# Reordering the last stage of a fused pair-update and mixture-of-experts kernel: transposes by halves, an earlier gate, a later bias

## What is computed

```
a    = layernorm(layernorm(x))
left = mask * (a @ Wl.T + bl) * sigmoid(a @ Wlg.T + blg)        # right likewise
t    = einsum('ikc,jkc->ijc', left, right);  t = layernorm(t)
x    = x + (t @ Wo.T + bo) * sigmoid(a @ Wg.T + bg)
p    = softmax(layernorm(x) @ router_w + router_b)              # 8 experts
top2 = the two largest p, divided by their sum
x    = x + sum over the top2 of p_e * (layernorm(x) @ expert_w[e] + expert_b[e])
```

## Time and profile before

| what | value |
|---|---|
| median of 3 runs | 1064.48 us (1064.04 to 1065.31) |
| the profiled execution | 1064.93 us |
| its span, first to last instruction | 1063.1 us |
| busy over the span: TensorE, VectorE, GpSimd, ScalarE | 90%, 78%, 62%, 42% |
| mean granted TensorE clock | 0.972 |
| first `turns` of stage C | at 342.7 us |
| last `total` | at 1058.5 us |

### The profile page before, as it was taken

How to read it: one execution, slowest core, us unless ns; L and a number is a source line. 1 busy time by engine, 2 the same in 40 slices (tenths; PEclk the granted TensorE clock), 3 DMA queues, 4 the chain that set the end, 5 groups by cost and what they waited for, 6 DMA issues and landing times.

```text
span 1063.1 us, 20940 instructions
## 1 busy us (share of the span) xinstructions
PE 957.2 (90%) x6712; PEld 545.5 (51%) x6712; DVE 829.9 (78%) x2945; ACT 448.5 (42%) x842; POOL 661.0 (62%) x632
## 2 busy tenths in 40 slices
PE   4798999979999689999999999999999999999986
PEld 3566666768886444444444444444444444444432
DVE  4899999831224678888888888888888888888883
ACT  1465566611111234444444444444444444444433
POOL 5997888432221137676767676767676767676654
PEclk9999999989999569999999999999999999999999
DMA  7678777989980123242424242423242423242331
GB/s 186 199 255 280 277 260 250 349 274 312 301 255 31 31 74 97 80 121 80 120 81 119 80 119 81 120 80 120 80 120 80 120 81 120 80 119 80 100 90 59
DMA packets 119390, 153.07 MB, mean 144 GB/s; under 512 B 10486, under 2 KB 76278, under 8 KB 117238
## 3 DMA queue, kind: packets, MB, share of 16 engines
q1 hardware_dynamic: 118150, 151.32, 46.2%
q10 hardware_dynamic: 1136, 0.46, 0.2%
HBM read 67.33 MB, written 50.33 MB: 111 GB/s over the span
## 4 chain that ended last, share of the span: by engine, by line
PE 44%; DVE 42%; issue 6%; POOL 5%; DMA 1%; ACT 1%; SPq 0%; POOLq 0%; DVEq 0%
PE b_m L773 13%; PE ein L666 11%; DVE zb L997 8%; PE gt L706 6%; PE ring L760 6%; DVE stage L834 6%; DVE bst_x L1046 4%; PE pr_a L629 4%; DVE sig_c L1006 3%; DVE x2t L1013 3%; DVE bst L821 3%; DVE bst_t L895 2%; POOL xs L378 1%; POOL xs L382 1%; PE xt_a L617 1%
## 5 line engine op out<-in xcount | busy, mean ns | idle before, releaser
L442 POOL TENSOR_TENSOR zb<-bcs,x2d 128x512 f32<-128x512 f32 x256 | 326.6, 1276 | 216.3 <-ACT bcs L549 162.9
L773 PE MATMUL b_m<-zb,w_exp 128*64 128x512 f32 x1024 | 258.7, 614 | 1.1 <-POOL zb L442 1.1
L549 ACT ACTIVATE bcs<-ring 128x512 f32<-128x512 f32 x256 | 153.7, 601 | 208.0 <-PE ring L760 202.0
L997 DVE TENSOR_TENSOR zb<-ring,x2d 128x512 f32<-128x512 f32 x256 | 175.7, 686 | 57.6 <-PE ring L760 57.0
L834 DVE SCALAR_TENSOR_TENSOR stage<-pr_a,mt,sig_a 128x128 f32<-128x128 f32 x512 | 148.0, 420 | 11.2 <-ACT sig_a L493 11.2
L760 PE MATMUL ring<-wt,sel 64*128 64x512 f32 x512 | 128.3, 498 | 26.8 <-DVE zb L997 26.6
L629 PE MATMUL pr_a<-w_proj,xts 64*128 64x256 f32 x1024 | 139.3, 402 | 14.4 <-DVE stage L834 13.9
L427 POOL TENSOR_TENSOR tn<-t_all,rr 128x512 f32<-128x512 f32 x64 | 85.8, 1340 | 60.8 <-PE gt L687 32.8
L773 PEld LDWEIGHTS b_m<-zb,w_exp 128*64 128x64 f32 x1024 | 57.7, 135 | 119.8 <-issue 95.2
L629 PEld LDWEIGHTS pr_a<-w_proj,xts 64*128 64x128 f32 x1024 | 96.1, 191 | 43.0 <-issue 22.1
L493 ACT ACTIVATE sig_a<-pr_a 128x512 f32<-128x512 f32 x128 | 76.4, 597 | 72.1 <-PE pr_a L629 72.0
(11 more groups left out here) (132 smaller groups left out, 1495.7 us busy)
## 6 DMA issues: line engine op xcount, KB each, us to landing
left_right_scratch<-stage SPq DMA_DIRECT2D x16, 2048.0 KB, 7.6
x2d<-x2t SPq DMA_DIRECT2D x256, 128.0 KB, 2.8
chunk<-left_right_scratch SPq DMA_DIRECT2D x24, 1024.0 KB, 9.0
xc<-in_x SPq DMA_DIRECT2D x64, 256.0 KB, 3.1
out<-outc SPq DMA_DIRECT2D x64, 256.0 KB, 2.1
chunk<-left_right_scratch SPq DMA_DIRECT2D x12, 384.0 KB, 8.1
chunk<-left_right_scratch SPq DMA_DIRECT2D x8, 192.0 KB, 5.4
chunk<-left_right_scratch SPq DMA_DIRECT2D x4, 256.0 KB, 8.0
```

The lines of the kernel that those rows point to most:

```text
L442: pool.tensor_tensor(zb[:, tile_buffer(u, m), :], bcs[:, n % 2, :], x2d[:, u % 2, m % 2, :], ALU.mult)\
L549: act.activation(bcs[:, n % 2, :], ring[:, m % 2, :], ACT.Copy).then_inc(bcast_out, 1)
L773: ins = pe.matmul(b_m[rows[t], :], w_exp[:, ep, :], zb[:, tile_buffer(u, 2 * ep + t), :], start=ep == 0, stop=ep == EP - 1, skip_group_che ...
L997: dve.tensor_tensor(zb[:, tile_buffer(u, m), :], ring[:, m % 2, :], x2d[:, u % 2, m % 2, :], ALU.mult).then_inc(z_dve, 1)
```

## The change

All transposes of the last stage are done by halves of 64 partitions, half `r` into bank `r` of the target, as `turns` does already: `x_turn` (into `gt`), `y_turn` and `pack_turn` (now both into `b_d`, the latter behind `back`'s results in it). The readers (`residual`, `y_evacuate`, `pack`) read both banks. `turns` no longer waits for the pack; `y_turn`, `pack_turn` and `back` get the waits that the shared `b_d` needs.

TensorE's new order in slot `u` is: bcast 2, 3; back(v-1); x_turn(v); bcast 4, 5; expert 0, 1; in odd slots pack_turn; bcast 6, 7; turns(n); y_turn(u-1); bcast 0, 1 of `u+1`; bias; out_gate(n); expert 2, 3. So `out_gate(n)` stands ahead of the last two experts, and ScalarE's `gate(n)` and VectorE's `gated(n)` now run at the end of the same slot, no longer in the next one; `x_turn(v)` waits for `gated(v)`.

GpSimd: norm_x(n); scale 3, 5; norm_t(n+1); scale 7; scale 1 of `u+1`. ScalarE: bcast 3, 5; pack; bcast 7; copies(n); soft; bcast 1 of `u+1`; gate(n); y_evacuate(u-1).

VectorE in even slots: scale 2; route 1; back 1; route 2; back 0; route 3; scale 4; route 4; back 3; route 5; residual(v); route 6; back 2; scale 6; logits; route 7 to 10; bn 2; route 11; bn 3; route 12; scale 0; route 13; bn 0; route 14; bn 1; route 15; gated(v+1); route 16; total. In odd slots: route 17; scale 2; back 3; route 18; back 2; route 19; back 1; back 0; scale 4; route 20; logits; residual(v); rstd 1, 0, 2; scale 6; rstd 3 to 8; scale 0; bn 0, 3; rstd 9 to 11; bn 1, 2; gated(v+1); rstd 12; total. Its list in the diff below is cut, since this is all of it.

```diff
@@ -453,15 +453,15 @@
             ins.then_inc(sel_made, 1)
             for u in range(-LEAD - 1, UNITS):
                 n = u + LEAD + 1
+                if has(n) and n >= NX:
+                    norm_x(n)
                 if has(u):
                     scale(3, u)
                     scale(5, u)
-                if has(n) and n >= NX:
-                    norm_x(n)
+                if has(n + 1):
+                    norm_t(n + 1)
                 if has(u):
                     scale(7, u)
-                if has(n + 1):
-                    norm_t(n + 1)
                 if has(u + 1):
                     scale(1, u + 1)
 
@@ -519,12 +519,13 @@
                 chunk_b(c)
 
 
+            by_half = lambda ap: ap.rearrange("p (j r k) -> p r j k", j=JP, r=2)
+            by_bank = lambda ap: ap.rearrange("p r (j k) -> p r j k", j=JP)
+
             def copies(n):
                 act.wait_ge(turns_ready, n + 1)
                 if n >= 1:
                     act.wait_ge(og_ready, n)
-                by_half = lambda ap: ap.rearrange("p (j r k) -> p r j k", j=JP, r=2)
-                by_bank = lambda ap: ap.rearrange("p r (j k) -> p r j k", j=JP)
                 act.activation(by_half(xtn[:, :]), by_bank(gt[:, :, 0:N]), ACT.Copy)
                 act.activation(by_half(ttn[:, :]), by_bank(gt[:, :, N:2 * N]), ACT.Copy).then_inc(turns_out, 1)
 
@@ -539,7 +540,7 @@
                 h = u % 2
                 if u >= 2:
                     act.wait_ge(out_stored[h], u // 2 * 16)
-                act.activation(outc[:, h, :, :].rearrange("p j c -> p (j c)"), b_d[:, 0, :], ACT.Copy).then_inc(y_out, 1)
+                act.activation(outc[:, h, :, :].rearrange("p (j t) c -> p t j c", t=2), by_bank(b_d[:, :, 0:N]), ACT.Copy).then_inc(y_out, 1)
 
             def bcast(m, u):
                 n = tiles_before(POOL_TILES, u, m)
@@ -555,26 +556,25 @@
 
             def pack(s):
                 act.wait_ge(pack_turned, s + 1)
-                act.activation(wt[:, s % 2, :], gt[:, 1, :], ACT.Copy).then_inc(pack_out, 1)
+                act.activation(by_half(wt[:, s % 2, :]), by_bank(b_d[:, :, N:2 * N]), ACT.Copy).then_inc(pack_out, 1)
 
             for u in range(-LEAD - 1, UNITS + 1):
                 v, n = u + LEAD, u + LEAD + 1
                 if has(u):
                     bcast(3, u)
-                if has(v):
-                    gate(v)
-                if has(u):
                     bcast(5, u)
-                if u % 2 == 0 and has(u + 2):
-                    soft((u + 2) // 2)
                 if u % 2 == 1 and has(u + 1):
                     pack((u + 1) // 2)
                 if has(u):
                     bcast(7, u)
                 if has(n):
                     copies(n)
+                if u % 2 == 0 and has(u + 2):
+                    soft((u + 2) // 2)
                 if has(u + 1):
                     bcast(1, u + 1)
+                if has(n):
+                    gate(n)
                 if has(u - 1):
                     y_evacuate(u - 1)
 
@@ -683,21 +683,18 @@
             pairs = [slice(j * P, j * P + P) for j in range(JP)]
             rows = [slice(r * C, r * C + C) for r in range(2)]
 
-            def turn_half(bank, at, src):
-                return pe.transpose(gt[:, bank, at:at + C], src, ident[rows[bank], rows[bank]])
+            def turn_half(dst, r, at, src):
+                return pe.transpose(dst[:, r, at:at + C], src, ident[rows[r], rows[r]])
 
             def turns(n):
                 pe.wait_ge(norm_ready, n + 1)
                 pe.wait_ge(x_norm, n + 1)
                 if n >= 1:
                     pe.wait_ge(x2_ready, n)
-                u = n - LEAD - 1
-                if u % 2 == 1 and has(u + 1):
-                    pe.wait_ge(pack_out, (u + 1) // 2 + 1)
                 for part, src in enumerate((xn, tn)):
                     for j in range(JP):
                         for r in range(2):
-                            m = turn_half(r, part * N + j * C, src[rows[r], 2 * j:2 * j + 2, :].rearrange("p j c -> p (j c)"))
+                            m = turn_half(gt, r, part * N + j * C, src[rows[r], 2 * j:2 * j + 2, :].rearrange("p j c -> p (j c)"))
                 m.then_inc(turns_ready, 1)
 
             def out_gate(n):
@@ -709,9 +706,10 @@
                 o.then_inc(og_ready, 1)
 
             def x_turn(v):
-                pe.wait_ge(gate_ready, v + 1)
+                pe.wait_ge(om_done, v + 1)
                 for j in range(JP):
-                    m = pe.transpose(gt[:, 0, pairs[j]], xc[:, v % XC, 2 * j:2 * j + 2, :].rearrange("p j c -> p (j c)"), ident)
+                    for r in range(2):
+                        m = turn_half(gt, r, j * C, xc[rows[r], v % XC, 2 * j:2 * j + 2, :].rearrange("p j c -> p (j c)"))
                 m.then_inc(x_turned, 1)
 
             def y_turn(u):
@@ -719,16 +717,21 @@
                 pe.wait_ge(back_done, min(u + LEAD + 1, UNITS))
                 if u >= 1:
                     pe.wait_ge(y_out, u)
+                if u % 2 == 0 and has(u + 2):
+                    pe.wait_ge(pack_out, u // 2 + 2)
                 for j in range(JP):
-                    m = pe.transpose(b_d[:, 0, pairs[j]], x2t[:, u % X2, pairs[j]], ident)
+                    for r in range(2):
+                        m = turn_half(b_d, r, j * C, x2t[rows[r], u % X2, pairs[j]])
                 m.then_inc(y_turned, 1)
 
             def pack_turn(s):
                 pe.wait_ge(pick_step, (s + 1) * PICK_OPS)
-                pe.wait_ge(om_done, min(2 * s + LEAD, UNITS))
+                pe.wait_ge(back_done, min(2 * s + LEAD - 1, UNITS))
+                if s >= 2:
+                    pe.wait_ge(y_out, 2 * s - 2)
                 for j in range(JP):
-                    m = pe.transpose(gt[:, 1, pairs[j]],
-                                     pk[:, 4 * j:4 * j + 4, :, :].bitcast(F32).rearrange("p t z n -> p (t z n)"), ident)
+                    for r in range(2):
+                        m = turn_half(b_d, r, N + j * C, pk[rows[r], 4 * j:4 * j + 4, :, :].bitcast(F32).rearrange("p t z n -> p (t z n)"))
                 m.then_inc(pack_turned, 1)
 
             def back(w):
@@ -737,6 +740,8 @@
                     pe.wait_ge(back_done, w)
                 if has(w - LEAD - 1):
                     pe.wait_ge(y_out, w - LEAD)
+                elif w == LEAD - 1:
+                    pe.wait_ge(pack_out, 1)
                 for j in range(JP):
                     for t in range(2):
                         m = pe.matmul(b_d[:, t, j * BACK:(j + 1) * BACK], x2t[rows[t], w % X2, pairs[j]], route[rows[t], :],
@@ -781,32 +786,32 @@
                     bcast(3, u)
                 if has(v - 1):
                     back(v - 1)
+                if has(v):
+                    x_turn(v)
                 if has(u):
                     bcast(4, u)
                     bcast(5, u)
                     expert(0, u)
                     expert(1, u)
-                if has(v):
-                    x_turn(v)
                 if u % 2 == 1 and has(u + 1):
                     pack_turn((u + 1) // 2)
-                if has(u):
-                    bias(u)
-                if has(u - 1):
-                    y_turn(u - 1)
                 if has(u):
                     bcast(6, u)
                     bcast(7, u)
                 if has(n):
                     turns(n)
+                if has(u - 1):
+                    y_turn(u - 1)
                 if has(u + 1):
                     bcast(0, u + 1)
                     bcast(1, u + 1)
                 if has(u):
+                    bias(u)
+                if has(n):
+                    out_gate(n)
+                if has(u):
                     expert(2, u)
                     expert(3, u)
-                if has(n):
-                    out_gate(n)
 
 
         @block.vector
@@ -1005,12 +1010,15 @@
                 dve.wait_ge(og_ready, v + 1)
                 dve.scalar_tensor_tensor(sig_c[:, :], gt[:, 1, :], og_bias[:, 1:2], sig_c[:, :], ALU.add, ALU.mult).then_inc(om_done, 1)
 
+            by_half = lambda ap: ap.rearrange("p (j r k) -> p r j k", j=JP, r=2)
+            by_bank = lambda ap: ap.rearrange("p r (j k) -> p r j k", j=JP)
+
             def residual(v):
                 dve.wait_ge(om_done, v + 1)
                 dve.wait_ge(x_turned, v + 1)
                 if v >= X2:
                     dve.wait_ge(y_turned, v - X2 + 1)
-                dve.tensor_tensor(x2t[:, v % X2, :], gt[:, 0, :], sig_c[:, :], ALU.add).then_inc(x2_ready, 1)
+                dve.tensor_tensor(by_half(x2t[:, v % X2, :]), by_bank(gt[:, :, 0:N]), by_half(sig_c[:, :]), ALU.add).then_inc(x2_ready, 1)
 
             def norm_x(v):
                 dve.wait_ge(xc_in[v % XC], v // XC * 16 + 16)
...
```

More of the change, by code:

```diff
@@ L890, in _, with stats_t @@
             dve.wait_ge(ein_dve, C // 2)
-            def stats_t(s, js):
+            def stats_t(s, js, last):
                 for j in js:
```

(146 more changed lines are left out.)

9 lines of the change are left out of this document (4 added, 5 removed).

## The result

The changed kernel takes 1006.22 us (median of 4 runs, 1005.70 to 1007.34) against 1064.89 before, a ratio of 0.945 (95% interval 0.9434 to 0.9467). 1003.5 was predicted, with a range of 993 to 1025. The span of its profiled execution is 1004.3 us, 58.8 less: 1.0 up to slot 1, 54.1 in slots 1 to 57, 3.7 from slot 58 on.

The account below looks back on a forecast made before the run. TensorE and VectorE, both nearly full, wait for each other in turn. Slots of 9.61 for 10.63 us save 58 over 57 slots, the last five 3: 1063.1 - 61 + 1.8 = 1003.9, less 0.45: 1003.5, range 993 to 1025.

Parts of the forecast that it names:

- The loop: Stage C, once a slot: TensorE takes 3.84 us from tile 6 read to tile 2 ready, VectorE's scale 2 to 6 the rest, 6.3.
- The walk of a slot: Step-by-step timing of TensorE and VectorE in an even and an odd slot: 19.22 us per pair, 9.61 a slot against 10.63.
- The copies: ScalarE's copies ahead of out_gate: done by 6.2 and 6.7 us against 6.76, hidden, in odd slots with nothing to spare.
- Halves: x_turn, y_turn and pack_turn on TensorE: 0.25 us each by halves against 0.41 to 0.56 whole, removing 0.55 us per slot.
- The rival's price: Halves do not overlap: eight loads one behind another, 0.84 us a transpose instead of 0.25, 1088 us in all; chance 0.04.
- Two banks: VectorE's residual reading two banks: unchanged at 0.68 us, the lower bound; upper bound 1.36.
- VectorE 2% from the bound: VectorE's busy time, 9.39 us per slot, leaves the forecast slot of 9.61 only 2% above it.
- the 96 put down as a sign: Sign listed in the prediction: VectorE over 96% busy, with no idle before scale 2.
- the rival did not come in: VectorE becomes the bound: dearer residual or dependent small steps make a slot 9.8 to 10.1 us, 1014 to 1031; chance 0.25.
- Covers: Work on other engines expected hidden: norm_t by 0.7 us, norm_x ahead of scale 3 by 0.4, doublings with slack 1.3.
- TensorE's wait before y_turn: Sign: TensorE idle before y_turn in even slots, some 0.6 us, and hardly elsewhere.
- wait that was named as a sign of being wrong: A new wait in every slot: TensorE for GpSimd's zb or the copies, or VectorE before scale 0 for transfers.

Follow-up runs that it names:

- the old list: The changed kernel with VectorE's old order of work put back, only gated(v+1) kept ahead of total: 1113.05 us, ratio 1.0451.
- the halves alone: The kernel before with all transposes by halves and their waits, every order as it was: 1088.69 us, ratio 1.0224.
- the late gate: The changed kernel with out_gate behind experts 2, 3, gate and gated in the next slot, x_turn behind experts 0, 1: 1096.36 us, ratio 1.0290.
- the early bias: The changed kernel with the bias ahead of bcast 6, 7 again: 1031.80 us, ratio 0.9685.
- GpSimd's old list: The changed kernel with GpSimd's order scale 3, 5, norm_x, scale 7, norm_t, scale 1: 1022.78 us, ratio 0.9598.
- the logits moved: The changed kernel with logits ahead of scale 6 in even slots: 999.17 us, ratio 0.9382.
- the new list: The changed kernel, VectorE reordered: even slots residual behind route 4, logits ahead of scale 6, statistics between small steps; odd scale 2 first, statistics between rstd: 1001.47 us.

## Why the prediction was right

- **The loop.** That VectorE's work between scale 2 and scale 6, with TensorE's piece behind it, set a slot before is shown by the old list (slots of 11.0 and 10.8 when it is put back) and by y_turn alone by halves (3 us of 17). The order makes most of the gain (with x_turn and y_turn whole the kernel is already at 1028), and in it their halves are worth 22 us.
- **The walk of a slot.** For even and odd slots 9.64 and 9.58 were walked and 9.65 and 9.70 measured, 9.68 over slots 1 to 57: 54 us for 58. In even slots two terms ahead of y_turn were each 0.10 too long (bcast 2, 3 with back 1.18, not 1.28; experts 0, 1 1.87, not 1.97), which is lost again in the waits: turns wait for residual, which the walk had in time by 0.06, and y_turn waits for the logits, whose end was right (5.31 for 5.35). In odd slots the walk is 0.12 short. Rows of TensorE's timeline, then of ScalarE's: the copy of tile 7, which stands behind the pack in its list:

```profile
694.59 0.58 PE L765 MATMUL ring<-wt,sel 64*128 64x512 f32 x2
695.10 0.50 PE L770 MATMUL b_m<-wt,bias_hi 128*128 128x512 f32 x1
```

```profile
694.03 0.59 ACT L550 ACTIVATE bcs<-ring 128x512 f32<-128x512 f32 x1
```

bcast 1 needs that copy, ended at 694.62, so bcast 0, 1 take 0.51 to the next start and not 0.43; the walk had only tile 6 there. The bias adds 0.04 in both slots (0.66 to 0.67, not 0.62). The copies, called hidden "with nothing to spare", do release out_gate last in odd slots, but it starts no later behind the bias than in even ones. Ahead of slot 1 1.0 was gained where 0 was put down, and from slot 58 to the end 3.7 for 3.
- **Luck.** The total came within 2.7 us, but five of the eleven expectations of the runs above, worked out in the same way, missed by 14 to 59 us (the halves alone, the old list, the late gate, the early bias, GpSimd's old list). They had left out a new wait, a lateness handed on to the next slot, or the clock. In the change itself the waits that the walk had missed are only 0.1 to 0.2 us each, and partly fall where TensorE waits anyway. That so small an error was left is luck in part.
- **Halves.** 0.25 was right (0.25 to 0.28). The Trainium skill ("TensorE: Matmul & The Clock Gate", LDWEIGHTS) prices a load by its columns, not its rows, and the trace agrees: one load takes 138 ns at 64 rows and 140 at 128. The rival's price, eight loads one behind another, is not seen, and the overlap of other row groups that the page allows (Part 3, The mechanism) is.
- **Two banks.** residual 683 ns against 681: the lower bound, as taken.
- **VectorE 2% from the bound.** It is 95.8% busy, a little under the 96 put down as a sign, and the rival did not come in: with the logits moved a slot still got 0.14 shorter on average (9.54). It is near, though. With the logits ahead VectorE idles only 0.28 a pair of slots in the stretch read (714.62), and each reordering that made it later in one slot paid in the next (the bias, the new list).
- **Covers.** norm_t is hidden, as walked, and so are the doublings. That norm_x stood ahead of scale 3 was walked as harmless; it is worth 16.6 us, and the prediction did not say so. Nor did it see that all the halves, with pack_turn's move to `b_d`, cost 23 us without the new order. Of the other signs, TensorE's wait before y_turn is 0.37, not some 0.6, and no wait that was named as a sign of being wrong stands on TensorE or VectorE in the slots shown.

## What to carry to other kernels

When two engines are each 90% full, look in the chain for the loop between them, and move everything that has slack to the other side of it; savings inside one engine's idle time bring little until then (3 us of 17 here), and about their full price afterwards (22 us, 20 worked out). A change made of several moves can't be split by undoing one: here the pieces that cost anything when undone cost 17 to 107 us each (22, 107, 90, 26, 17), 262 in sum, where all together bring 59. Before moving a result to another buffer, list what its new neighbour makes it wait for, as pack_turn had to wait for the logits in `b_d`.

## What had not been expected of the hardware

With VectorE's old list, the granted clock fell to 0.50 again and again in the middle of steady work, in 16 of 57 slots, with no idle time of TensorE above 1.6 us in the slot shown. The longest falls cost a slot 3 us (14.05 against 10.99), the others 1.3 to 1.8. It also fell three times in the trace of the kernel before with y_turn by halves; that of the kernel before has no fall in slots 1 to 57. One trace of each does not show that the saving brought the falls. A small step (128x128) on VectorE that reads the output of the one before it starts 0.32 us after that one's start (703.88 to 704.20); where the next step is independent it starts after 0.20 (704.93 to 705.13).
